# Row maxima of the first heads spread over two projection blocks, head 0's row sent within the projection, and the last stores taken off the border

## What is computed

```python
xn = _layernorm(x)
q = _split_heads(xn @ q_w.T + q_b, 16) / sqrt(32)
k = _split_heads(xn @ k_w.T + k_b, 16)
v = _split_heads(xn @ v_w.T + v_b, 16)
attn = softmax(einsum('bhqd,bhkd->bhqk', q, k))
ctx = einsum('bhqk,bhkd->bhqd', attn, v)        # back to (b, s, 512)
h = xn @ weight @ aux_weight1 @ aux_weight2
out = x + (ctx @ out_w.T + out_b) + tanh(h + bias)
```

## Time and profile before

| | us |
|---|---|
| median of 3 runs | 4177.87 |
| lowest and highest | 4174.76, 4183.38 |
| span of the profiled execution | 4167.9 |
| PE busy in it | 4078.0 (98%) |
| POOL busy | 3253.1 (78%) |
| DVE busy | 3127.0 (75%) |
| ACT busy | 2356.4 (57%) |

### The profile page before, as it was taken

The page is one execution under the profiler, slowest core; times in us unless marked ns, Lnnn a source line. Parts: engine busy times, 40 slices in busy tenths (PEclk is TensorE's granted clock), DMA queues, the critical chain, the costliest instruction groups (busy, mean ns, idle before and its releaser), DMA issues.

```text
span 4167.9 us, 77711 instructions
## 1 busy us (share of the span) xinstructions
PE 4078.0 (98%) x21216; PEld 2490.3 (60%) x21216; DVE 3127.0 (75%) x5058; ACT 2356.4 (57%) x4515; POOL 3253.1 (78%) x1180
## 2 busy tenths in 40 slices
PE   8999999889999999999999999999999999999999
PEld 6888888645555555555555555555555555555467
DVE  4443334668888888888888888888888888888454
ACT  2221222157676666666676666666666767666621
POOL 1222222179999999999999999999999999999930
PEclk9999999999999999999999999999999999999999
DMA  4444445368878888888888888878888888888787
GB/s 169 162 161 160 151 160 166 122 141 174 172 165 176 176 175 176 171 172 175 173 174 178 177 170 173 171 168 175 176 177 173 175 172 171 176 176 174 154 260 263
DMA packets 246352, 722.11 MB, mean 173 GB/s; under 512 B 87392, under 2 KB 88416, under 8 KB 184544
## 3 DMA queue, kind: packets, MB, share of 16 engines
q0 software_dynamic: 55296, 402.68, 49.8%
q1 hardware_dynamic: 107648, 201.88, 14.2%
q10 hardware_dynamic: 83040, 113.01, 9.8%
HBM read 178.00 MB, written 136.31 MB: 75 GB/s over the span
## 4 chain that ended last, share of the span: by engine, by line
PE 53%; DMA 14%; issue 7%; ACT 3%; POOL 2%; ACTq 0%; POOLq 0%; SPq 0%; DVE 0%; DVEq 0%
PE sm_bank L948 16%; PE st_bank L964 16%; PE pv_bank L970 16%; DMA dma_sum<-pool_sum 10%; DMA dma_sum<-probs 3%; ACT probs L781 3%; PE sm_bank L235 3%; PE sm_bank L970 1%; POOL pool_sum L716 1%; PE st_bank L235 1%; POOL ctx_out L741 0%; DMA q_stack<-s_y 0%; PE sm_bank L957 0%; DMA q_stack<-max_row 0%; POOL dma_sum L727 0%
## 5 line engine op out<-in xcount | busy, mean ns | idle before, releaser
L862 DVE TENSOR_REDUCE part_max<-sm_bank 128x1 f32<-128x512 f32 x4016 | 2442.3, 678 | 412.3 <-PE sm_bank L948 406.0
L716 POOL TENSOR_TENSOR pool_sum<-pool_sum,probs 128x2048 f32<-128x2048 f32 x512 | 2504.9, 4892 | 16.7 <-ACT probs L781 0.9
L781 ACT ACTIVATE probs<-st_bank 128x512 f32<-128x512 f32 x3840 | 1959.4, 616 | 608.6 <-PE st_bank L964 580.6
L964 PE MATMUL st_bank<-q_stack,k_stack 97*128 97x512 f32 x4096 | 1648.4, 403 | 19.2 <-ACT probs L781 8.3
L948 PE MATMUL sm_bank<-k_stack,q_stack 96*128 96x512 f32 x4016 | 1655.1, 412 | 3.0 <-issue 2.7
L948 PEld LDWEIGHTS sm_bank<-k_stack,q_stack 96*128 96x128 f32 x4016 | 763.3, 190 | 550.7 <-DVE part_max L862 334.1
L964 PEld LDWEIGHTS st_bank<-q_stack,k_stack 97*128 97x128 f32 x4096 | 779.9, 191 | 274.8 <-ACT probs L781 128.0
L970 PE MATMUL pv_bank<-probs,v_pair 128*32 128x512 f32 x7680 | 936.0, 602 | 0.0
L970 PEld LDWEIGHTS pv_bank<-probs,v_pair 128*32 128x32 f32 x7680 | 204.9, 110 | 455.7 <-ACT probs L781 262.9
L727 POOL DMA_DIRECT2D dma_sum<-probs x320 | 348.3, 1088 | 70.7 <-ACT probs L781 26.2
L356 POOL TENSOR_TENSOR y_out<-y_out,x_in 128x512 f32<-128x512 f32 x64 | 82.6, 1291 | 406.9 <-ACT y_out L388 401.1
(11 more groups left out here) (100 smaller groups left out, 2431.4 us busy)
## 6 DMA issues: line engine op xcount, KB each, us to landing
dma_sum<-probs POOLq DMA_DIRECT2D x320, 1024.0 KB, 8.3
dma_sum<-pool_sum POOLq DMA_DIRECT2D x64, 1024.0 KB, 10.3
q_stack<-s_q_hi ACTq DMA_DIRECT2D x122, 256.0 KB, 6.6
k_stack<-s_k_hi ACTq DMA_DIRECT2D x122, 256.0 KB, 4.8
x_in<-in_x SPq DMA_DIRECT2D x16, 1024.0 KB, 7.7
s_q_hi<-qk_hi SPq DMA_DIRECT2D x16, 1024.0 KB, 4.3
s_q_lo<-qk_lo SPq DMA_DIRECT2D x16, 1024.0 KB, 6.5
s_k_hi<-qk_hi SPq DMA_DIRECT2D x16, 1024.0 KB, 4.3
```

What stands on the lines that cost most here:

```text
L716: nc.gpsimd.tensor_tensor(total[:], one[:], tile_at(r, kt)[:], ALU.add).then_inc(pool_added, 1)
L781: nc.scalar.activation(tile_at(r, kt)[:, q * BLK:(q + 1) * BLK], st_bank[:, st_place(kt * QB + q)], ACT.Exp, scale=SCALE).then_inc(probs_r ...
L862: nc.vector.tensor_reduce(part_max[:, k:k + 1], sm_bank[:, sm_place(k)], AX.X, ALU.max).then_inc(max_scores_read, 1)
L964: nc.tensor.matmul(st_bank[:, st_place(u)], k_st[r][0:ROWS + 1, kt * P:(kt + 1) * P], q_st[r][0:ROWS + 1, q * BLK:(q + 1) * BLK], start=Tr ...
```

## The change

- The 80 score tiles are spread. `early_maxima(n, u)` gives the tiles of unit `u` of block `n`: none before block 14, four each in units 10 to 15 of block 14, four each in units 0 to 7 of block 15, three each in units 8 to 15. The first four wait for DVE's last reads of the transposes in `turned` (`xt_lo_ready`).
- Head 0's row is made in the projection. In unit 13 of block 15 PE transposes `row_max` into one slot of `turned` (all later tiles move on by one slot, `early_slot`), DVE negates it, and SP sends it to `q_stack` from within the projection.
- Block 15 computes y before v (`y_first`), so v units are its last.
- SP's list changes: head 2's stacks and the first `v_pair` are loaded behind block 14 (their SBUF is that of the transposed input of even blocks and of `xn`, which are no longer needed then); the row stands behind block 15's y stores; the last v store stands at the end, and neither it nor the y stores are awaited at the border. ACT waits for v before it loads head 3, and SP waits for v and y before head 61's last loads.
- One memset of a row of ones moves from attention to the projection.

The diff, cut to its core (unchanged helpers, renamed tiles and the like are left out):

```diff
+MAX_FROM = 10
+TURN_AT = 13
+BLOCK_UNITS = 2 * CT + 2 * JT
+def early_maxima(n, u):
+    if not isinstance(n, int) or n < BLOCKS - 2:
+        return range(0)
+    if n == BLOCKS - 2:
+        return range(4 * (u - MAX_FROM), 4 * (u - MAX_FROM) + 4) if u >= MAX_FROM else range(0)
+    first = 4 * (BLOCK_UNITS - MAX_FROM) + 4 * min(u, 2 * CT) + 3 * max(u - 2 * CT, 0)
+    return range(first, first + (4 if u < 2 * CT else 3))
+TURN_SLOT = early_maxima(BLOCKS - 1, TURN_AT)[0]
+V_STORED, Y_STORED = PRIME + DMA * BLOCKS, PRIME + DMA * (BLOCKS - 1) + JT * DMA
+def early_slot(k):
+    return k + (k >= TURN_SLOT)
...
 # projection, sync
-                sp.wait_ge(proj_free, PRIME + n * UNITS + 2 * CT + JT)
-                sp.dma_start(tokens(dram["v"], n), v_out[:]).then_inc(v_stored, DMA)
-                if isinstance(n, int) and n == BLOCKS - 1:
+                if not y_first(n):
+                    sp.wait_ge(proj_free, PRIME + n * UNITS + v_unit(n) + JT)
+                    sp.dma_start(tokens(dram["v"], n), v_out[:]).then_inc(v_stored, DMA)
+                if y_first(n):
                     for j in range(JT):
                         sp.wait_ge(y_ready, n * JT + j + 1)
                         sp.dma_start(tokens(dram["y"], n)[:, j], y_out[:, j]).then_inc(y_stored, DMA)
+                    sp.wait_ge(row_negated, 1)
+                    sp.dma_start(first["q_stack"][MROW:MROW + 1, :].bitcast(F32),
+                                 first["max_row"][:].bitcast(F32)).then_inc(first["row_loaded"], DMA)
+                    sp.wait_ge(proj_free, PRIME + n * UNITS + v_unit(n) + JT)
+                    sp.dma_start(tokens(dram["v"], n), v_out[:]).then_inc(v_stored, DMA)
...
-            for par in range(2):
-                body(BLOCKS - 2 + par, par, False)
+            body(BLOCKS - 2, 0, False)
+            load_head(sp, dram, 2, first["q_stack2"], first["k_stack2"], first["loaded2"])
+            load_v(sp, dram, 0, first["v_pairs"][:, 0], first["v_loaded"])
+            body(BLOCKS - 1, 1, False)
             for s in qk_stored:
                 sp.wait_ge(s, PRIME + 2 * DMA * BLOCKS)
-            sp.wait_ge(v_stored, PRIME + DMA * BLOCKS)
-            sp.wait_ge(y_stored, PRIME + DMA * (BLOCKS - 1) + JT * DMA)
 # projection, gpsimd
+                else:
+                    pool.wait_ge(y_ready, n * JT)
+                    nc.gpsimd.memset(first["k_stack2"][MROW:MROW + 1, :].bitcast(F32), 1.0).then_inc(ones_ready, 1)
 # projection, vector
-                for k in range(BESIDE * u, BESIDE * u + BESIDE):
+                for k in early_maxima(n, u):
...
+                if u == TURN_AT:
+                    dve.wait_ge(row_turned, 1)
+                    nc.vector.tensor_scalar(first["max_row"][:], turned[0:QT, TURN_SLOT % CT, 0:P], -1.0, None,
+                                            ALU.mult).then_inc(row_negated, 1)
...
+                for part in ((y_sums, v_sums) if y_first(n) else (v_sums, y_sums)):
+                    part(n)
 # projection, tensor
+                if isinstance(n, int) and n == BLOCKS - 1 and u == TURN_AT:
+                    pe.wait_ge(row_ready, 1)
+                    pe.wait_ge(max_read, TURN_SLOT - CT + 1)
+                    nc.tensor.transpose(turned[0:QT, TURN_SLOT % CT, 0:P], first["row_max"][:],
+                                        keep["ident"][:]).then_inc(row_turned, 1)
+                for k in early_maxima(n, u):
...
-                    if k >= CT:
-                        pe.wait_ge(max_read, k - CT + 1)
-                    nc.tensor.matmul(turned[:, k % CT], first[queries][0:ROWS, q * P:(q + 1) * P],
+                    slot = early_slot(k) - CT
+                    if slot < 0:
+                        pe.wait_ge(xt_lo_ready, (BLOCKS - 1) * CT + k + 1)
+                    elif slot == TURN_SLOT:
+                        pe.wait_ge(row_negated, 1)
+                    else:
+                        pe.wait_ge(max_read, slot + 1 - (slot > TURN_SLOT))
+                    nc.tensor.matmul(turned[:, early_slot(k) % CT], first[queries][0:ROWS, q * P:(q + 1) * P],
 # attention, sync
-            load_v(sp, dram, 0, v_sb[0], v_loaded[0])
-            load_row(0, 0)
-            load(2, 2)
             load_row(1, 1)
...
                 if more == 2:
+                    sp.wait_ge(first["v_stored"], V_STORED)
+                    sp.wait_ge(first["y_stored"], Y_STORED)
 # attention, scalar
                 exps(0, 0, kt)
+                if kt == LOAD_AT[0]:
+                    act.wait_ge(first["v_stored"], V_STORED)
 # attention, vector
-            negate(0)
+            dve.sem_inc(max_row_ready, 1)
 # attention, tensor
-            turn_max(0, False)
-            pe.wait_ge(max_row_ready, 1)
+            pe.sem_inc(turned_ready, 1)
```

108 lines of the change are left out of this document (62 added, 46 removed).

## The result

The changed kernel takes 4141.69 us (median of 4 runs, 4140.18 to 4147.64), the kernel before, run beside it, 4176.32 (4 runs, 4171.67 to 4183.38). The ratio is 0.9916 (95% interval 0.9899 to 0.9933), which is 35 us off, between 28 and 42. The forecast was 4146.3, its range 4140 to 4155. The profiled execution after took 4140.99 us, with a span of 4139.2. Against the profiled execution before, whose span was 4167.9, that is only 28.7 us. So two numbers have to be explained: why the profiles differ by 28.7 where the forecast said 31.6, and why the medians differ by 35.

A forecast was written before the change was run, and what follows sets the result against it. TensorE, busy 98% of 4167.9 us, was taken as the bound, with waits to remove. 17.9 + 11.1 + 2.6 = 31.6 us off gave 4136.3; plus 10.0 from profile to median, 4146.3 us, range 4140 to 4155.

The forecast's parts named there:

- Term 1: Blocks 14 and 15: spreading the maxima tiles ends TensorE's waits for VectorE's reads, 17.9 us saved (14 to 18.2).
- The wait for head 0's load: Before tile 0 in block 14, TensorE newly waits for head 0's load; 4 us of cover expected.
- Term 2: Border from projection to attention: 13.94 us shrinks to 2.88, 11.1 us saved.
- The sum of 2.88 us: New border, last projection matmul to head 0's score: 0.43 + 0.72 + 0.37 + 1.12 + 0.24 us.
- Term 3: Clock behind the border: 14 matmuls no longer run at 1.2 GHz, 2.6 us saved; with a drop 1.0.
- the new gap is nearer to the first: Border's 2.4 us idle resembles the 2.19 us gap ahead of 53.97, clock staying 1.00, more than the 2.67 us gap.
- The rival with the drop: Clock drops at the border, saving 1.0 us there instead of 2.6; 30.0 us in all, 4147.9 us; chance 0.27.
- risk of a slower loop: Attention's moved tiles slow its loop; 0.50 us per head loses the gain, 0.7 gives 4190; chances 0.01, 0.03, 0.03.
- The 10.0 us between profile and median: Median of the runs shown lies 10.0 us above the profile; added to 4136.3 to give 4146.3 us.
- TensorE's start-up: Rival at the border: beginning new code costs 2.7 us and the clock's 1.6; 27.3 us saved, 4150.6 us; chance 0.09.
- The row was not late: Rival at the border: head 0's row is late, TensorE waits up to 5.1 us, 4151 us; chance 0.03.
- the maxima did not stall: Rival in blocks 14 and 15: 22 units keep half of each wait, 9.5 us lost, 4156 us; chance 0.06.

The follow-up runs named there:

- the spread alone: Kernel before with only head 0's 80 maxima tiles spread as in the changed kernel; 4156.55 us, ratio 0.9956.
- late row: Changed kernel with the DMA of head 0's row issued when attention starts, not within the projection; 4142.49 us in one run, border 6.58 us.
- awaited stores: Changed kernel with the border's waits for the v and y stores put back; 4139.83 us in one run, border 7.46 us.
- the border alone: Changed kernel without the spread, all 80 tiles in block 15, five a unit, negation one unit sooner; 4160.27 us, ratio 0.9963.
- five early: Changed kernel with five tiles a unit over 16 units from unit 10 of block 14; one run, last block 105.08 us, border 3.27 us.
- the kernel before aligned: Kernel before with 32 unused bytes so transposed blocks and outputs start at a multiple of 64 bytes; 4168.29 us, ratio 0.9982.
- control: Kernel before with 64 unused bytes, tiles moved but still 32 bytes past a multiple of 64; one run, 46.53 us a block.
- aligned: Changed kernel with 32 unused bytes, so the second set of transposed blocks and the outputs also start at multiples of 64; 4138.64 us, ratio 0.9915.
- Four in every unit: Changed kernel with four tiles in each of 20 units from unit 12 of block 14; one run, last block 87.50 us, border 3.29 us.
- filled kernel: Changed kernel with seven more matmuls of unused result behind the last projection unit; 4147.52 us, ratio 0.9936.

## Why the prediction was right, and where it was not

**What bounds the kernel** held. TensorE is busy 98% as before, all that was saved ahead of attention reached the end, and GpSimd's first sums of heads 0 and 63 are still 48.81 us a head apart (831.50 and 3906.83).

**Term 1, 17.9 us**: 18.2 in the traces (of which some 0.3 are the shorter v and y units of block 14), 17.9 with the spread alone, 18.0 from the kernel with only the border changed. Blocks 14 and 15 were to take 52 and 57.7 us and take 51.8 and 58.0. The step on which it stood, that the fourth read is ready 0.1 us ahead of the weights that need its bank, held with 4.13 us for the forecast 4.07. Five reads fail in either block, which is the same reckoning with one read more. The wait for head 0's load is in no list.

**Term 2, 11.1 us**: 10.7 from the two profiles. The sum of 2.88 us was short by 0.36. The step that failed is that SyncE passes its waits and the barrier at no cost of its own: the store ends at 817.89 and the issue in the chain begins only at 818.38, 0.49 us that the sum does not have. Against that, from there to TensorE's first instruction it is 0.87 us for the 1.12 taken, and from the first score to the transposed one 0.34 for 0.24. In the chain:

```profile
818.38 0.79 issue
...
819.25 0.50 PE sm_bank L1015
```

The old border was 13.12 to 13.94 us in four traces, mainly since the row's DMA varies, and the term was read from the dearest of the four. By the mean of the four (13.5) it is 10.3.

**Term 3, 2.6 us**, was wrong. The clock falls: 14 matmuls in 4.5 us at 0.62. The failed step is "the new gap is nearer to the first", the one of 2.19 us without a fall. The gap of 2.19 us is itself followed by a fall in 11 of 14 traces. Only the kernel before's, and those of the late row and of the awaited stores, show 1.00 behind it. The rival with the drop (0.27) was the true case, at 1.0 us for the forecast's 2.6. And of that 1.0 it is open how much arrives: head 0 is 104.2 to 107.3 us long with the old border and 105.2 to 107.5 with the new one (in the mean 106.1 for both), and with no fall at the border it was 105.8. These traces also differ at the loop's entry, within head 0. The idle time of 2.44 to 2.74 us there was followed by a fall in ten of the fourteen, and by none in the spread alone, the border alone, five early and the kernel before aligned. The first of these, where the clock at the entry was 0.57 and 0.56 in the kernels before and after:

```profile
863.50:867.30 3.80, 3.72 (x15) 2.67 (x16) 3.21 (x6) 2.83 (x6) 3.80 (x3) 1.00 0.71 140
```

Compared like with like, head 0 with a fall at both places takes 107.3 and 107.2 us with the old border (the kernel before and its control) and 106.0, 105.8 and 106.0 with the new one (the changed kernel twice, and aligned), 1.3 us less. (Four in every unit, at 107.5, had the lower clock at the entry for twice as long.) Without a fall at the entry it takes 104.2 and 105.5 with the old border and 106.3 and 105.2 with the new one, nothing less. In the filled kernel 0.6 us of it was left at the loop's entry (31.4 us behind the last projection matmul for 32.0) and none at `ctx_out`. What takes it up was not settled; TensorE's waits for ScalarE's `probs` and the fall at the loop's entry lie between. So term 3 was worth 0 us in the mean of all traces and 1.3 us in those that are most alike.

**The term that was missing** is the tiles' place. The forecast named the new places as a risk of a slower loop and saw no gain in them: eight blocks of 0.42 us, 3.4 us, and no line of the diff is about it.

**The sum.** 18.0 + 10.3 + 0 + 3.4 = 31.7 us, with 0 for the clock, against the 32.6 (26.7 to 38.4) of the five runs and the 35 (28 to 42) of the first measurement. That the forecast's 31.6 came to the same is luck: two errors cancel, 2.6 for the clock and 0.8 of border against 3.4 for the place.

**The 10.0 us between profile and median** were carried over as a constant, and they are none. In every run whose span is on record, the time lies 1.8 to 1.9 us above it. So the profiled execution of before took about 4169.7 us (an estimate from its span), and of the 31 timed executions of that kernel on record only two were quicker (4168.36 and 4168.94). It was a quick one in places that other executions fix: no fall of the clock at 54 us, 1.5 us less than in eleven of the others, and 3319.3 us of attention where the same loop takes 3317.5 to 3325.9 in the other 13 traces. The profiled execution after had a late start and both early falls, and lies 0.7 us below its median. The execution before lies 6.6 below the 4176.32 of its four runs, and 28.7 + 6.6 - 0.7 = 34.6 is the difference of the medians. Against the forecast of 4146.3, the profiles brought 2.9 us less than the 31.6, and the step from profile to median was 2.5 us and not 10.0; together the time came out 4.6 us under the forecast, inside the range. With 10.0 for that step too it would have been 4149.2, inside the range as well.

**The other rivals**: TensorE's start-up does not show at the border (2.51 us idle, all with a releaser), and does at the loop's entry (2.46 us `<-issue`, as in the earlier trace rows), as it did before; the forecast had already counted it in the span. The row was not late, the maxima did not stall, the loop was not slower.

## What to carry to other kernels

When one engine serves another through n banks, write down the time of the n-th read against the weight load that needs its bank; one read too many in a unit costs a wait in each unit, and spreading the same reads costs nothing. At a border between stages, list what is in series there (the last unit's longest tail, a store awaited, a small transfer issued late): each was worth 3 to 4 us alone here, and they added up. When tiles change their place, note whether each starts at a multiple of 64 bytes before and after; and compare stages, not whole executions, when an effect is smaller than the spread.

## What the runs showed of the hardware

**A start address 32 bytes past a multiple of 64 costs a stationary operand 2%.** A v or y unit of 12 matmuls, whose weights are 128x128 pieces of such a tile, takes 2.80 us instead of 2.75, with the matmuls following each other at 0.233 us instead of 0.229; a unit that streams the tile as the moving side takes 2.81 for 2.80, and 2.80 too in the control, where the tile is 32 bytes past as well. Over 16 blocks this is 7.5 us, and 32 unused bytes give it back.

**Idle times of one length come out unlike.** Fourteen traces have the same gap of 2.18 to 2.20 us ahead of the projection; behind it the granted clock fell in eleven and stayed at 1.00 in three. Each fall costs 1.5 us: 16.8 us from the first projection matmul to the first `rstd` without it, 18.3 with it. The new border's 2.5 us was followed by a fall in all six traces that have it, 1.08 us in one trace by none, and the 2.44 to 2.74 us at the loop's entry by a fall in ten traces and by none in four. In the weights stage the wait for `raw_a` does the same to the 32 matmuls behind it. The first row is the kernel before's, the second the changed kernel's:

```profile
14.78 13.97 PE L226 MATMUL w_bank<-raw_a,a_t 128*128 128x512 f32 x32 [2.13 <-DMA raw_a<-in_a]
```

```profile
14.95 15.67 PE L252 MATMUL w_bank<-raw_a,a_t 128*128 128x512 f32 x32 [2.01 <-DMA raw_a<-in_a]
```

The shorter wait was followed by the fall (15.67 us), the longer one was not (13.97), and this is 1.7 of the 1.87 us by which the changed kernel's projection began later. In other traces it fell behind waits of 2.16, 2.35 and 4.25 us, and stayed up behind 1.16, 1.42, 1.46, 2.51, 2.73, 2.85, 2.87 (twice) and 3.19. The Trainium skill (TensorE: Matmul & The Clock Gate, Part 1: The HAM clock gate) says that the monitor runs free of the program; the traces agree, with like gaps on both sides.

**One loop, 3317.5 to 3325.9 us.** The loop over heads has the same instructions in all fourteen traces. The spread grows along it: GpSimd's 16th `ctx_out` comes 836.4 to 840.5 us behind the first transposed score, the 63rd 3134.2 to 3143.2. TensorE's waits for `dma_sum` are 28.9 to 34.5 us in all and follow the length only in part (29.8 us with the shortest loop, 33.9 with the longest, but 34.5 at 3322.9 and 29.8 also at 3323.6). Most of it can be read from two figures of each trace, from the first transposed score on: TensorE's idle time, 49.0 to 57.1 us in all, and the time at the lower of the clock's two levels, 27.3 to 45.8 us. Taking the first and half of the second off the whole (3317.5 to 3325.9, 8.4 us between the extremes) leaves 3249.2 to 3253.1, 3.9 between them. Why the falls and the waits differ from one execution to the next stays open, and this is most of the spread between runs.
